# The attention stage of a macaron block: loops written out, the exponentials' scale in a register, another order of the maximum pass

## The chip, the cores and the metric

One NeuronCore of a Trainium2 chip runs the whole program. The time is device microseconds of one execution, first to last instruction plus the little that lies around them; the metric is the median of several executions.

## What is computed

x has 2 x 2048 tokens of width 256. The block is a half-weighted feed-forward layer, causal attention with 16 heads of 16, and the same feed-forward layer again, each behind a layer norm:

```python
x = x + 0.5 * ffn(layernorm(x))
x = x + attention(layernorm(x))      # B=2, S=2048, 16 heads of DK=16, causal, softmax, output projection + bias
x = x + 0.5 * ffn(layernorm(x))      # ffn: [x,-x] -> 1024 -> 1024 -> 256, weights +-1
```

## The kernel before

The program has three stages that share one set of PSUM tiles: A (first feed-forward layer, then q, k, v, which go to scratch memory in HBM), B (attention) and C (context and output projection, second feed-forward layer). The change is in stage B alone, which runs from about 475 to 1298 us of the span.

Stage B works on 16 pairs of heads (2 batches x 8). A pair has 4 query chunks of 512 (QCH); chunk i takes 2i+2 steps, 20 steps in all (STEPS): steps 0-1 are chunk 0, 2-5 chunk 1, 6-11 chunk 2, 12-19 chunk 3. A step has four slots j = 0..3: two key blocks of 128 times two heads. For each slot `scores` (L1201) makes four matmuls of 32 columns each side by side into one of three PSUM banks (`ffn_mm` 0 to 2), ACT makes the exponential (L1161) with a scale that it reads from SBUF, `exp_scale[:, 0:1]`, and writes `probs`. POOL masks the diagonal blocks (L1114). Three steps later (PV_LAG) `products` (L1222) multiplies the four slots with v in fp32 and adds into the fourth bank; PV_POINTS says after which slot of a step. When a chunk's last products are done, ACT copies the context out (L1150, `evacuate`) and SP stores it (L1066).

The softmax needs each row's maximum. It comes from a second pass over q and k, the maximum pass: 40 "units" of 128 queries x 512 keys a pair (`pe_item`, L568, and L573 for the diagonal's mask), into two PSUM tiles used in turn (`ffn_tr`, `ffn_acc`); DVE reduces each (L588, `dve_item`). After a chunk's last unit DVE makes the negated maxima as columns; a "turn" transposes them on PE (L577), DVE casts them to `m_row` (L601), and SP copies `m_row` into the two shift rows of q with two DMAs (`sp_rows`, L607). Turns are called T0 to T3 here, by chunk. `scores` of chunk i wait at their first slot for the rows of Ti: `rows_in`, 32 for each turn, counted over all pairs.

The maximum pass runs ahead: while pair p's scores run, the units of its later chunks and of pair p+1's first chunks are made. OWN_POINTS and AHEAD_POINTS say after which slot (4 x step + slot) each item comes; where products stand at the same slot, the item comes behind them. LEAD = 21 units of the first pair are made before stage B's scores begin.

q, k and v of pair p+1 come by `load_pair` (L302 to L305): 16 DMAs for q and k, one for v, into the other of two buffers, once the last products of pair p-1, which read that buffer, are done. SP works its queue in order. In one pair that order is written by hand: the rows of T2, then the load, then the stores and the other turns:

```python
order = [turns[0], "load", 0, 1, turns[1]] + turns[2:3] + [2] + turns[3:4] + [3]
for x in order:
    if x == "load":
        wait(sp, se.pv_done, pair * STEPS)
```

In the last pair the load is that of the first context chunk (`load_ctx`, 8 DMAs, L480), which DVE (`normalize`, L1279 to L1286) takes up behind its last turn; the second context chunk is loaded when that is done.

The code is a body of two pairs: body 0 stands alone, bodies 1 to 6 are a hardware loop on each engine (`Fori`), body 7 stands alone. In the loop, thresholds of semaphores are computed from the loop's register.

Of the kernel before, what the change touches and what calls it, by code (L numbers as in the profile page):

```python
# [22 lines left out]
U32 = mybir.dt.uint32  # L23
ALU = mybir.AluOpType
# [4 lines left out]
P = 128  # L29
# [4 lines left out]
CH = 512  # L34
# [15 lines left out]
BODY_PAIRS = 2  # L50
BODIES = BATCH * PAIRS // BODY_PAIRS
# [4 lines left out]
LEAD = 21  # L56
# [192 lines left out]
def build(nc, x, w_q, w_k, w_v, w_o, b_o, k0, k1, k2, s0, s1, s2, out):  # L249
# [8 lines left out]
    with ExitStack() as top:  # L258
# [239 lines left out]
        def with_turns(lo, hi):  # L498

            seq = []  # L500
            for n in range(lo, hi):
                seq.append(units[n])
                seq += [("turn", i) for i in range(QCH - 1) if last_unit[i] + TURN_DELAY[i] == n]
            return seq

        AHEAD = with_turns(0, LEAD)
        OWN = with_turns(LEAD, UNITS) + [("turn", QCH - 1)]
        assert len(AHEAD) == len(AHEAD_POINTS) and len(OWN) == len(OWN_POINTS)
        assert len(AHEAD) + len(OWN) == S_USES and S_USES % 2 == 0
# [17 lines left out]
        def schedule(u, last):  # L527

            plan = [[] for _ in range(4 * STEPS)]
            work = [(u, x) for x in OWN] + [(1 - u, x) for x in AHEAD]  # L530
            for use, ((buf, x), point) in enumerate(zip(work, OWN_POINTS + AHEAD_POINTS)):
                if buf == u or not last:
                    plan[point].append((buf, x, use))
            return plan

# [3 lines left out]
        body_steps = [(u, s) for u in range(BODY_PAIRS) for s in range(STEPS)]  # L539
        LOAD_STEP = AHEAD_POINTS[0] // 4  # L540
        OUT_PROJ_STEP = STEPS - 6
        EXPS, NSTEP = 4 * len(body_steps), len(body_steps)

        def bank(k):

            return 1 if k == EXPS - 1 else k % ST_BANKS

        def bank_free(k):

            return next(n for n in range(k - 1, k - EXPS, -1) if bank(n % EXPS) == bank(k)) + 1  # L550
# [503 lines left out]
        with ExitStack() as st:  # L1054
# [7 lines left out]
            @block.sync  # L1062
            def _(sp):
                def store(pair, n, i):
                    wait(sp, se.ctx_done, n + 1)
                    sp.dma_start(ctx_scr[bass.ds(pair, 1), :, i * CH:(i + 1) * CH].rearrange("o p n -> (o p) n"),  # L1066
                                 ctx_out[:, i % 2, :]).then_inc(ctx_st[i % 2], 16)

                def body(it, last):
                    for u in range(BODY_PAIRS):  # L1070
                        pair = it * BODY_PAIRS + u
                        base = pair * S_USES + len(AHEAD)
                        turns = [(b, x[1], use) for step in schedule(u, last and u == 1) for b, x, use in step if x[0] == "turn"]
                        order = [turns[0], "load", 0, 1, turns[1]] + turns[2:3] + [2] + turns[3:4] + [3]
                        for x in order:
                            if x == "load":
                                wait(sp, se.pv_done, pair * STEPS)
                                if last and u == 1:
                                    load_ctx(sp, 0, 0)
                                else:  # L1080
                                    load_pair(sp, 1 - u, pair + 1)
                                continue
                            if last and u == 1 and x == QCH - 2:
                                wait(sp, sc.ctx_n, 1)
                                load_ctx(sp, 0, 1)
                            if isinstance(x, int):
                                store(pair, pair * QCH + x, x)
                            else:
                                sp_rows(sp, x[0], x[1], base + x[2])
# [4 lines left out]
                body(0, False)  # L1094
                with sp.Fori(1, BODIES - 1) as it:
                    body(it, False)
                body(BODIES - 1, True)
                for sem in ctx_st:
                    sp.wait_ge(sem, 8 * BATCH * PAIRS * QCH)

            @block.gpsimd
            def _(pool):
                def body(it):
                    for g, (u, s) in enumerate(body_steps):
                        if not diagonal(s):
                            continue
                        i = chunk_of[s]
                        for par in range(2):
                            kb, _, c0 = step_slots(s)[2 * par]
                            w = (kb - TPC * i + 1) * P - c0  # L1110
                            pool.wait_ge(se.exp_done, it * EXPS + 4 * g + 2 * par + 2)
                            pool.sem_inc(se.gate_pool, 1)
                            view = probs[:, g % P_SLOTS, 2 * par:2 * par + 2, c0:c0 + w]
                            nc.gpsimd.affine_select(out=view, in_=view, compare_op=ALU.is_ge, fill=0.0,  # L1114
                                                    base=c0 - (kb - TPC * i) * P, pattern=[[0, 2], [1, w]],
                                                    channel_multiplier=-1).then_inc(se.mask_done, 1)

                with pool.Fori(0, BODIES - 1) as it:
                    body(it)
                body(BODIES - 1)  # L1120

            @block.vector
            def _(dve):
# [3 lines left out]
                def body(it, last):  # L1127
                    for u in range(BODY_PAIRS):
                        pair = it * BODY_PAIRS + u
                        for step in schedule(u, last and u == 1):  # L1130
                            for buf, x, use in step:
                                i = x[1] if x[0] == "turn" else x[1] // TPC
                                owner = pair if buf == u else pair + 1
                                dve_item(buf, x, pair * S_USES + len(AHEAD) + use, (len(AHEAD) + use) % 2, owner * QCH + i)

                with dve.Fori(0, BODIES - 1) as it:
                    body(it, False)
                body(BODIES - 1, True)

            @block.scalar  # L1140
            def _(act):
                ends = [g + PV_LAG for g, (u, s) in enumerate(body_steps) if s + 1 == STEPS or chunk_of[s + 1] != chunk_of[s]]

                def body(it, first=False, last=False):
                    def evacuate(n, body=0):

                        stored = BODY_PAIRS * QCH * 8
                        wait(act, se.pv_done, it * NSTEP + (body * NSTEP + ends[n] - PV_LAG + 1))
                        wait(act, ctx_st[n % 2], it * stored + (body * stored + n // 2 * 16))
                        nc.scalar.activation(ctx_out[:, n % 2, :], ctx_ps[:, :], ACT.Copy).then_inc(se.ctx_done, 1)  # L1150

                    for g, (u, s) in enumerate(body_steps):
                        for j, (kb, h, c0) in enumerate(step_slots(s)):
                            k = 4 * g + j
                            if first and k == 4 * (P_SLOTS - 1):
                                act.wait_ge(sa.qk_st, NCH * 128)
                                act.wait_ge(sa.v_st, NCH * 64)
                            if j == 0:
                                wait(act, se.pv_done, it * NSTEP + (g - P_SLOTS + 1))
                            wait(act, se.st_ready, it * EXPS + k + 1)  # L1160
                            nc.scalar.activation(probs[:, g % P_SLOTS, j, c0:CH], st_ps[bank(k)][:, c0:CH], ACT.Exp,  # L1161
                                                 scale=exp_scale[:, 0:1]).then_inc(se.exp_done, 1)
                            if j == PV_POINTS[s] and g in ends:
                                evacuate(ends.index(g))
                            if j == PV_POINTS[s] and g + NSTEP in ends and not first:
                                evacuate(ends.index(g + NSTEP), -1)
                    if last:
                        act_ln_sqrt(ln3, 0)
# [248 lines left out]
```

## Time and profile before

| | |
|---|---|
| median of 3 runs | 1689.33 us (1683.36 to 1690.95) |
| profiled execution, its own time | 1687.42 us |
| its span | 1685.7 us |
| PE busy | 1610.8 us (96%) |
| DVE busy | 1158.1 us (69%) |
| ACT busy | 948.2 us (56%) |
| mean granted TensorE clock | 0.984 |

In stage B PE, DVE and ACT are all near full in most slices of the span; outside it PE alone is. A busy PE is not PE at its peak: matmuls overlap, and so the distance between the starts of two of them, not their length, is what one costs.

### The profile page before, as it was taken

The numbers are of one execution on the slowest core, as the hardware profiler recorded it, in microseconds if no ns is written. First come the engines' busy times: TensorE is split into PE (matmuls) and PEld (weight loads), VectorE is DVE, ScalarE is ACT, GpSimd is POOL, SyncE is SP. The second block draws the span as 40 slices with busy tenths as digits, with TensorE's granted clock in tenths as the row PEclk, the third lists the DMA queues.
The fourth block names the chain that finished last, engine by engine and source line by source line (L and its number), as shares of the span: only waits on it lengthen the run. The fifth ranks groups of instructions, "written<-read, shape, count | busy, mean of one in ns | idle before, by whom it ended". The sixth has DMA issues, their size and how long they took to land.

```text
span 1685.7 us, 40071 instructions
## 1 busy us (share of the span) xinstructions
PE 1610.8 (96%) x14224; PEld 731.9 (43%) x14224; DVE 1158.1 (69%) x1746; ACT 948.2 (56%) x1703; POOL 160.1 (9%) x320
## 2 busy tenths in 40 slices
PE   6899999999989999898999999999997899999998
PEld 3455555555533333333333333333332455555554
DVE  6545543454589888787887878878886556666632
ACT  2223223232279999797997989889997222222211
POOL 5200000000011111111111111111110000000000
PEclk9999999999999999999999999999999899999999
DMA  5011013110131112220122202222213111113000
GB/s 172 0 51 50 0 50 87 50 36 14 49 104 50 37 51 65 59 65 26 49 65 59 65 30 51 59 60 63 59 44 102 51 51 50 50 50 110 15 12 13
DMA packets 115790, 89.42 MB, mean 53 GB/s; under 512 B 76080, under 2 KB 95152, under 8 KB 115632
## 3 DMA queue, kind: packets, MB, share of 16 engines
q1 hardware_dynamic: 115632, 87.20, 18.0%
q8 instruction: 113, 1.85, 0.5%
q14 instruction: 45, 0.37, 0.1%
HBM read 49.15 MB, written 37.75 MB: 52 GB/s over the span
## 4 chain that ended last, share of the span: by engine, by line
PE 87%; DVE 3%; issue 3%; ACT 2%; DMA 2%; SPq 2%; DVEq 0%; ACTq 0%
PE ffn_mm L400 26%; PE ffn_mm L1201 16%; PE ffn_mm L1222 13%; PE ffn_mm L388 7%; PE ffn_acc L416 7%; PE ffn_acc L568 5%; PE ffn_tr L568 5%; PE ffn_mm L667 3%; PE ffn_acc L679 2%; ACT probs L1161 2%; PE ffn_acc L488 1%; PE ffn_tr L375 1%; PE ffn_tr L573 1%; DVE qk L1282 1%; DMA qk<-ctx_scr 1%
## 5 line engine op out<-in xcount | busy, mean ns | idle before, releaser
L1161 ACT ACTIVATE probs<-ffn_mm,exp_scale 128x512 f32<-128x512 f32 (+3 forms) x1280 | 705.5, 641 | 96.4 <-PE ffn_mm L1201 90.7
L1201 PE MATMUL ffn_mm<-qk 66*32 66x512 f16 (+7 forms) x5120 | 413.5, 359 | 25.2 <-issue 19.9
L588 DVE TENSOR_REDUCE m_part<-ffn_acc 128x2 f32<-128x1024 f32 (+1 forms) x314 | 351.2, 1119 | 76.4 <-PE ffn_acc L568 44.1
L400 PE MATMUL ffn_mm<-ffn_h1h,w 128*128 128x512 f16 x1024 | 389.4, 380 | 7.5 <-DVE ffn_h2l L453 7.5
L400 PE MATMUL ffn_mm<-ffn_h1l,w 128*128 128x512 f16 x1024 | 389.2, 380 | 0.0
L588 DVE TENSOR_REDUCE m_part<-ffn_tr 128x2 f32<-128x1024 f32 (+3 forms) x326 | 328.0, 1006 | 28.6 <-PE ffn_tr L573 15.4
L1222 PE MATMUL ffn_mm<-probs,v 128*32 128x512 f32 (+3 forms) x2560 | 307.7, 538 | 2.3
L446 ACT ACTIVATE ffn_h2h<-ffn_mm 128x512 f16<-128x512 f32 x128 | 76.2, 598 | 309.2 <-PE ffn_mm L400 294.5
L1201 PEld LDWEIGHTS ffn_mm<-qk 66*32 66x32 f16 (+1 forms) x5120 | 131.5, 94 | 252.3 <-ACT probs L1161 136.0
L453 DVE SCALAR_TENSOR_TENSOR ffn_h2l<-ffn_mm,ffn_h2h 128x512 f16<-128x512 f32 x128 | 86.3, 688 | 188.5 <-ACT ffn_h2h L446 188.5
L1114 POOL TENSOR_SCALAR_AFFINE_SELECT probs<-probs 128x256 f32<-128x256 f32 (+1 forms) x256 | 108.0, 422 | 734.8 <-ACT probs L1161 734.6
L400 PEld LDWEIGHTS ffn_mm<-ffn_h1h,w 128*128 128x128 f16 x1024 | 100.5, 98 | 126.0 <-DVE ffn_h2l L453 8.0
L446 ACT ACTIVATE ffn_h1h<-ffn_mm 128x512 f16<-128x512 f32 x128 | 76.5, 598 | 139.8 <-PE ffn_mm L388 139.8
L400 PEld LDWEIGHTS ffn_mm<-ffn_h1l,w 128*128 128x128 f16 x1024 | 100.5, 98 | 117.9 <-issue 1.3
L568 PE MATMUL ffn_acc<-qk 64*128 64x512 f16 (+1 forms) x628 | 117.3, 370 | 3.6 <-DVE m_part L588 2.8
L568 PE MATMUL ffn_tr<-qk 64*128 64x512 f16 (+3 forms) x652 | 114.5, 346 | 0.5
L416 PE MATMUL ffn_acc<-w,ffn_h2h 128*128 128x256 f16 x512 | 113.8, 273 | 0.3 <-DVE ffn_h2l L453 0.3
L416 PE MATMUL ffn_acc<-w,ffn_h2l 128*128 128x256 f16 x512 | 113.7, 273 | 0.0
L453 DVE SCALAR_TENSOR_TENSOR ffn_h1l<-ffn_mm,ffn_h1h 128x512 f16<-128x512 f32 x128 | 88.6, 692 | 35.6 <-ACT ffn_h1h L446 35.1
L388 PE MATMUL ffn_mm<-ffn_xh,w 128*128 128x512 f16 x256 | 99.3, 388 | 3.5 <-DVE ffn_xl L432 2.4
L388 PE MATMUL ffn_mm<-ffn_xl,w 128*128 128x512 f16 x256 | 99.2, 388 | 0.0
L1222 PEld LDWEIGHTS ffn_mm<-probs,v 128*32 128x32 f32 x2560 | 74.4, 110 | 32.9 <-ACT ctx_out L1150 8.1
(99 smaller groups left out, 1104.9 us busy)
## 6 DMA issues: line engine op xcount, KB each, us to landing
qk<-qk_scr SPq DMA_DIRECT2D x256, 64.0 KB, 2.6
ctx_scr<-ctx_out SPq DMA_DIRECT2D x64, 256.0 KB, 2.8
qk<-ctx_scr SPq DMA_DIRECT2D x64, 256.0 KB
v_scr<-v_pad SPq DMA_DIRECT2D x32, 256.0 KB, 2.9
v<-v_scr SPq DMA_DIRECT2D x16, 512.0 KB, 4.6
x_res<-L_attn_x SPq DMA_DIRECT2D x8, 512.0 KB, 3.8
qk_scr<-qk_hi SPq DMA_DIRECT2D x32, 128.0 KB, 1.8
qk_scr<-qk_lo SPq DMA_DIRECT2D x32, 128.0 KB, 1.8
```

Source lines behind the costliest of these rows:

```text
L388: ins = nc.tensor.matmul(f.mm[:, m % 4, :], w0[:, kt, m * P:(m + 1) * P], part[:, kt, :], start=(kt == 0 and part is f.xh), stop=(kt == DT ...
L400: ins = nc.tensor.matmul(f.mm[:, m % 4, :], w1[:, kt, m * P:(m + 1) * P], part[:, kt, :], start=(kt == 0 and part is f.h1h), stop=(kt == H ...
L416: ins = nc.tensor.matmul(f.acc[:, t // 2, t % 2 * D:(t % 2 + 1) * D], part[:, kt, t * P:(t + 1) * P], w2[:, kt, :], start=(kt == 0 and par ...
L446: nc.scalar.activation(dst[:, m, :], f.mm[:, m % 4, :], ACT.Relu).then_inc(hi, 1)
L453: nc.vector.scalar_tensor_tensor(out=dst[:, m, :], in0=f.mm[:, m % 4, :], scalar=0.0, in1=src[:, m, :], op0=ALU.max, op1=ALU.subtract).the ...
L568: ins = nc.tensor.matmul(s_ps[slot][:, h, 0:w], q_part(u, h, HEAD_ROWS[h], slice(t * P, (t + 1) * P)), k_part(u, h, HEAD_ROWS[h], slice(r ...
L588: nc.vector.tensor_reduce(m_part[u][:, t, :, r], s_ps[slot][:, :, 0:w], AX.X, ALU.max).then_inc(sb.s_done, 1)
L667: ins = nc.tensor.matmul(f.mm[:, j, :], w_t[:, j // DT, kt, j % DT * P:(j % DT + 1) * P], src[:, kt, :], start=(kt == 0), stop=(kt == DT - 1))
L1114: nc.gpsimd.affine_select(out=view, in_=view, compare_op=ALU.is_ge, fill=0.0, base=c0 - (kb - TPC * i) * P, pattern=[[0, 2], [1, w]], chan ...
L1161: nc.scalar.activation(probs[:, g % P_SLOTS, j, c0:CH], st_ps[bank(k)][:, c0:CH], ACT.Exp, scale=exp_scale[:, 0:1]).then_inc(se.exp_done, 1)
L1201: ins = nc.tensor.matmul(st_ps[bank(k)][c:c + 32, c0:CH], k_part(u, h, rows, slice(kb * P + c, kb * P + c + 32)), q_part(u, h, rows, slice ...
L1222: ins = nc.tensor.matmul(ctx_ps[row:row + 32, c0:CH], v_buf[u][:, kb, h * 32:(h + 1) * 32], probs[:, g % P_SLOTS, j, c0:CH], start=start, ...
```

## The change

- Stage B's hardware loops are gone: on every engine the 16 pairs are written out, and all semaphore thresholds are constants.
- ACT loads the scale once into a register, and the exponentials take it from there.
- The maximum pass has one table of 44 points for a pair. A point is 2 x (4 x step + slot) + late; an item with late = 0 comes ahead of the products of that slot, one with late = 1 behind them. LEAD is 24 (26 items are made ahead in place of 23), TURN_DELAY has a fourth number, PV_POINTS are others.
- SP has no order by hand: it goes through steps and slots, and at each slot first come the rows of a turn of that slot, then a store, then, at step 2's products, the load.

```diff
-LEAD = 21
+LEAD = 24
-PV_POINTS = (3, 1, 2, 1, 1, 0, 2, 1, 2, 1, 3, 2, 2, 1, 1, 0, 1, 2, 2, 2)
-TURN_DELAY = (2, 7, 3)
-OWN_POINTS = (1, 2, 3, 8, 9, 12, 13, 15, 15, 16, 19, 21, 22, 25, 27, 28, 29, 31, 33, 34, 39)
-AHEAD_POINTS = (39, 41, 41, 44, 46, 47, 51, 52, 52, 54, 56, 57, 59, 62, 63, 66, 68, 68, 71, 73, 75, 77, 77)
+PV_POINTS = (1, 1, 2, 1, 2, 1, 3, 2, 3, 2, 2, 0, 1, 0, 1, 0, 2, 2, 3, 1)
+TURN_DELAY = (2, 7, 4, 3)
+ITEM_POINTS = (5, 5, 14, 20, 22, 24, 24, 28, 32, 37, 41, 48, 49, 55, 55, 61, 67, 73, 73, 76, 77, 78, 78, 85,
+              89, 94, 95, 102, 102, 107, 111, 118, 119, 126, 129, 129, 138, 138, 143, 145, 145, 152, 152, 159)
...
+                for pair in range(ALL_PAIRS):
+                    last = pair == ALL_PAIRS - 1
+                    for s in range(STEPS + (PV_LAG if last else 0)):
+                        g = pair * STEPS + s
+                        for j in range(4):
+                            for _, owner, x, use in items(pair, s, j) if s < STEPS else ():
+                                if x[0] == "turn":
+                                    sp_rows(sp, owner % 2, x[1], use)
+                            if j == PV_POINTS[s % STEPS] and g in ends:
+                                n = ends.index(g)
+                                if last and n == len(ends) - 2:
+                                    wait(sp, sc.ctx_n, 1)
+                                    load_ctx(sp, 0, 1)
+                                store(n // QCH, n, n % QCH)
+                            if j == PV_POINTS[s % STEPS] and s == PV_LAG - 1:
+                                wait(sp, se.pv_done, pair * STEPS)
+                                if last:
+                                    load_ctx(sp, 0, 0)
+                                else:
+                                    load_pair(sp, 1 - pair % 2, pair + 1)
...
+                scale_now = act.alloc_register("exp_scale")
+                act.reg_load(scale_now, exp_scale[0:1, 0:1].bitcast(U32))
...
-                            nc.scalar.activation(probs[:, g % P_SLOTS, j, c0:CH], st_ps[bank(k)][:, c0:CH], ACT.Exp,
-                                                 scale=exp_scale[:, 0:1]).then_inc(se.exp_done, 1)
+                        nc.scalar.activation(probs[:, g % P_SLOTS, j, c0:CH], st_ps[bank(k)][:, c0:CH], ACT.Exp,
+                                             scale=scale_now).then_inc(se.exp_done, 1)
...
+                for g in range(ALL_STEPS):
+                    pair, s = divmod(g, STEPS)
+                    for j in range(4):
+                        scores(g, j)
+                        max_pass(pair, s, j, 0)
+                        if j == PV_POINTS[s] and g >= PV_LAG:
+                            products(g - PV_LAG)
+                        max_pass(pair, s, j, 1)
```

## Rows read from the trace of the kernel before

**Rows 1.** The windows view: pair 1, pairs 3 to 12, pair 14: length, busy by engine, PEclk.
```profile
526.18:575.41 49.23, 48.93 (x628) 17.50 (x624) 43.55 (x57) 45.43 (x86) 6.75 (x16) 1.00 0.20 56
625.60:1149.13 523.53, 501.36 (x6284) 178.05 (x6280) 435.67 (x561) 455.01 (x841) 67.47 (x160) 0.97 0.20 53
1198.44:1247.94 49.50, 49.12 (x632) 17.59 (x632) 43.39 (x57) 45.57 (x85) 6.75 (x16) 1.00 0.24 55
```

**Rows 2.** PE's timeline in a stretch without idle time.
```profile
824.30 0.39 PE L568 MATMUL ffn_acc<-qk 64*128 64x512 f16 x2
824.62 0.40 PE L1201 MATMUL ffn_mm<-qk 128*32 128x512 f16 x4
...
825.75 1.03 PE L1222 MATMUL ffn_mm<-probs,v 128*32 128x512 f32 x8
826.61 0.39 PE L1201 MATMUL ffn_mm<-qk 66*32 66x512 f16 x4
...
827.75 0.39 PE L568 MATMUL ffn_tr<-qk 64*128 64x512 f16 x2
827.98 0.38 PE L568 MATMUL ffn_acc<-qk 64*128 64x512 f16 x2
```

**Rows 3.** ACT's timeline where it runs without a break.
```profile
804.52 3.00 ACT L1161 ACTIVATE probs<-ffn_mm,exp_scale 128x512 f32<-128x512 f32 x5 [0.82 <-PE ffn_mm L1201]
807.39 0.62 ACT L1150 ACTIVATE ctx_out<-ffn_mm 128x512 f32<-128x512 f32 x1
807.87 5.51 ACT L1161 ACTIVATE probs<-ffn_mm,exp_scale 128x512 f32<-128x512 f32 x10
```

**Rows 4.** DVE's timeline, reductions one behind the other.
```profile
855.77 1.22 DVE L588 TENSOR_REDUCE m_part<-ffn_acc 128x2 f32<-128x1024 f32 x1
856.90 1.22 DVE L588 TENSOR_REDUCE m_part<-ffn_tr 128x2 f32<-128x1024 f32 x1
```

**Rows 5.** PE's timeline behind two idle stretches: start, length, instructions, idle before.
```profile
783.07 1.04 PE L1201 MATMUL ffn_mm<-qk 66*32 66x512 f16 x8 [4.37 <-issue]
...
1311.71 1.97 PE L375 MATMUL ffn_tr<-ident,ln_xn 128*128 128x128 f32 x8 [12.16 <-DVE ln_xn L367]
...
1320.64 0.38 PE L388 MATMUL ffn_mm<-ffn_xl,w 128*128 128x512 f16 x1
```

**Rows 6.** The view by line and form, stage B, ACT: busy us, mean ns.
```profile
L1161 ACT ACTIVATE probs<-ffn_mm,exp_scale 128x512 f32<-128x512 f32 x912 | 557.6, 703 | 48.6 <-PE ffn_mm L1201 47.0
...
L1150 ACT ACTIVATE ctx_out<-ffn_mm 128x512 f32<-128x512 f32 x63 | 38.6, 613 | 0.0
```

**Rows 7.** SP's queue in a pair of the loop and in pair 14.
```profile
842.01 0.35 SPq L1066 DMA_DIRECT2D ctx_scr<-ctx_out  x1
...
845.35 0.36 SPq L303 DMA_DIRECT2D qk<-qk_scr  x1
...
854.12 0.40 SPq L305 DMA_DIRECT2D v<-v_scr  x1
...
1207.41 1.30 SPq L607 DMA_DIRECT2D qk<-m_row  x2
1208.76 0.39 SPq L303 DMA_DIRECT2D qk<-qk_scr  x1
...
1216.13 0.42 SPq L305 DMA_DIRECT2D v<-v_scr  x1
```

**Rows 8.** PE's timeline of that loop pair: step 2's products.
```profile
840.35 0.60 PE L1222 MATMUL ffn_mm<-probs,v 128*32 128x256 f32 x7
```

**Rows 9.** The source view of L305: from issue to landing of v's load.
```profile
DMA to landing us min/median/max: 4.2/4.6/5.3
```

**Rows 10.** The chain of waits: landing of one turn's rows.
```profile
777.74 1.64 DMA qk<-m_row
```

**Rows 11.** A context load in SP's queue, and DVE's timeline where it is waited for.
```profile
1282.33 5.13 SPq L480 DMA_DIRECT2D qk<-ctx_scr  x8
...
1299.27 1.23 DVE L1279 TENSOR_TENSOR qk<-qk 128x1024 f32<-128x1024 f32 x1 [10.08 <-DMA qk<-ctx_scr]
```

More of the change, by code:

```diff
@@ L496, in build @@
         last_unit = {i: max(n for n, x in enumerate(units) if x[1] // TPC == i) for i in range(QCH)}
[L498 to L509, printed above, removed]
+        PERIOD, due = [], []
+        for n in range(2 * UNITS):
+            PERIOD.append((n // UNITS, units[n % UNITS]))
+            due += [(n + TURN_DELAY[i], n // UNITS, i) for i in range(QCH) if last_unit[i] == n % UNITS]
+            PERIOD += [(d, ("turn", i)) for at, d, i in due if at == n]
+        PERIOD = PERIOD[PERIOD.index((0, units[LEAD])):PERIOD.index((1, units[LEAD]))]
+        AHEAD = [x for d, x in PERIOD if d == 1]
+        assert len(PERIOD) == S_USES and len(ITEM_POINTS) == S_USES and S_USES % 2 == 0
         chunk_of = [i for i in range(QCH) for _ in range(2 * i + 2)]
@@ L525, in step_slots, with items @@
             return out
[L527 to L534, printed above, removed]
         def diagonal(s):
             return chunk_of[s] * TPC <= step_slots(s)[0][0]
-        body_steps = [(u, s) for u in range(BODY_PAIRS) for s in range(STEPS)]
-        LOAD_STEP = AHEAD_POINTS[0] // 4
+        ALL_STEPS = ALL_PAIRS * STEPS
         OUT_PROJ_STEP = STEPS - 6
-        EXPS, NSTEP = 4 * len(body_steps), len(body_steps)
+        EXPS = 4 * STEPS
+        def items(pair, s, j):
+            found, use = [], len(AHEAD) + pair * S_USES
+            for (d, x), point in zip(PERIOD, ITEM_POINTS):
+                if pair + d == ALL_PAIRS:
+                    continue
+                if point // 2 == 4 * s + j:
+                    found.append((point % 2, pair + d, x, use))
+                use += 1
+            return found
+        ends = [pair * STEPS + s + PV_LAG for pair in range(ALL_PAIRS) for s in range(STEPS)
+                if s + 1 == STEPS or chunk_of[s + 1] != chunk_of[s]]
         def bank(k):
-            return 1 if k == EXPS - 1 else k % ST_BANKS
+            return k % ST_BANKS
         def bank_free(k):
-            return next(n for n in range(k - 1, k - EXPS, -1) if bank(n % EXPS) == bank(k)) + 1
+            return k - ST_BANKS + 1
         EARLY = [0] * 15 + [1] * 3 + [0]
@@ L1067, in store @@
                                  ctx_out[:, i % 2, :]).then_inc(ctx_st[i % 2], 16)
[L1069 to L1089, printed above, removed]
                 sp_rows(sp, 0, 1, AHEAD.index(("turn", 1)))
@@ L1136, in _ @@
-                with dve.Fori(0, BODIES - 1) as it:
-                    body(it, False)
-                body(BODIES - 1, True)
+                for pair in range(ALL_PAIRS):
+                    for s in range(STEPS):
+                        for j in range(4):
+                            for _, owner, x, use in items(pair, s, j):
+                                i = x[1] if x[0] == "turn" else x[1] // TPC
+                                dve_item(owner % 2, x, use, use % 2, owner * QCH + i)
@@ L1140, in _ @@
             @block.scalar
             def _(act):
[L1142 to L1160, printed above, removed]
-                            nc.scalar.activation(probs[:, g % P_SLOTS, j, c0:CH], st_ps[bank(k)][:, c0:CH], ACT.Exp,
-                                                 scale=exp_scale[:, 0:1]).then_inc(se.exp_done, 1)
[L1163 to L1168, printed above, removed]
-                        for n, g in enumerate(ends):
-                            if g >= NSTEP:
-                                evacuate(n)
@@ L1178, in _ @@
+                act_ln_sqrt(ln3, 0)
+                evacuate(len(ends) - 1)
             @block.tensor
@@ L1249, in _, with scores @@
-                body(0, first=True)
-                with pe.Fori(1, BODIES - 1) as it:
-                    body(it)
-                body(BODIES - 1, last=True)
+                def scores(g, j):
+                    pair, s = divmod(g, STEPS)
+                    i = chunk_of[s]
+                    kb, h, c0 = step_slots(s)[j]
+                    k = 4 * g + j
+                    if j == 0 and s == first_step[i]:
+                        wait(pe, se.rows_in, (pair * QCH + i + 1) * 32)
+                    wait(pe, se.exp_done, bank_free(k))
+                    rows = ALL_ROWS[h]
+                    for c in range(0, P, 32):
+                        ins = nc.tensor.matmul(st_ps[bank(k)][c:c + 32, c0:CH], k_part(pair % 2, h, rows, slice(kb * P + c, kb * P + c + 32)),
+                                               q_part(pair % 2, h, rows, slice(i * CH + c0, (i + 1) * CH)), start=True, stop=True,
+                                               tile_position=(0, c))
+                    ins.then_inc(se.st_ready, 1)
@@ new lines, in max_pass @@
+                def max_pass(pair, s, j, after):
+                    for late, owner, x, use in items(pair, s, j):
+                        if late != after:
+                            continue
+                        if owner != pair and x == units[0]:
+                            load_wait(owner % 2, owner // 2)
+                        pe_item(owner % 2, x, use % 2, use - 1, owner * QCH + x[1] + 1 if x[0] == "turn" else None)
+                for g in range(ALL_STEPS):
+                    pair, s = divmod(g, STEPS)
+                    for j in range(4):
+                        scores(g, j)
[3 more added lines that the diff above has]
+                        max_pass(pair, s, j, 1)
+                    if pair == ALL_PAIRS - 1 and s == OUT_PROJ_STEP:
+                        wait(pe, se.s_done, ALL_PAIRS * S_USES)
+                        pe_out_proj(pe, 0, lambda j: None)
@@ L1255, in build @@
+                for g in range(ALL_STEPS - PV_LAG, ALL_STEPS):
+                    products(g)
         with ExitStack() as st:
@@ L1360, in free @@
                         elif m < ST_BANKS:
-                            wait(pe, sb.exp_done, BODIES * EXPS)
+                            wait(pe, sb.exp_done, ALL_PAIRS * EXPS)
                         else:
```

137 lines of the change are left out of this document (48 added, 89 removed).

## The prediction

> **What bounds the kernel now.** I looked first at the windows view, cut at the first exponential of each pair. A pair of straight code takes 49.2 to 49.5 us at full clock; PE is busy for 48.9 of them, DVE for 43.6, ACT for 45.4 [rows 1]. Three engines are close together, so the limit must be read from distances between starts. In PE's timeline a product step of 512 columns lasts until the next start 0.86 us, which is four passes of 0.215; a unit lasts 0.22 when another unit follows and 0.32 when a score does [rows 2]: going from a score or product to a unit, or back, costs 0.10 more each way. ACT's exponential of 512 columns costs (807.39 - 804.52)/5 = 0.574, its context copy 0.48 [rows 3]. DVE's full reduction costs 1.13 [rows 4].
>
> PE's floor for a pair: scores 58 slots of 512, 6 of 384, 8 of 256 and 8 of 128 columns, 14.7 us; products, 16 steps at 0.86 and 4 at 0.43, 15.5; units 28 x 0.215 + 12 narrow ones of 0.11 on average, 7.3; masks 16 x 0.11, 1.8; together 39.3. Laid out slot by slot, the tables before have 76 crossings between units and the rest: + 7.6 = 46.9. ACT's floor, each form at its length less the overlap of 0.13, is 58 x 0.574 + 6 x 0.47 + 8 x 0.35 + 8 x 0.24 + 4 copies x 0.48 = 42.7 (the narrower forms by 0.11 a 128 columns); DVE's is its busy 43.6 less the overlap of its records (1.22 long, 1.13 apart [rows 4]), about 42.3. Of 49.3, some 2.4 are then waits of PE where ACT or DVE is late for a moment.
>
> **The loops.** Ten pairs of the loop with five jumps back take 523.5 us [rows 1]; ten straight ones would take 493. The jumps cost 30.5: PE stands idle 4.37 us, waiting for nothing but its own issue [rows 5], and the granted clock falls behind it: 0.97 over these pairs, 1.00 over a straight one [rows 1]. Written out, the code has no jump, and straight pairs in the bodies at both ends show no such hole: -30.5. Register arithmetic on the queues goes too; it is hidden behind work.
>
> **The register.** The exponential that reads its scale from SBUF lasts 703 ns, the context copy of the same shape, without an operand in SBUF, 613 [rows 6], and the starts differ by the same 0.09 [rows 3]. No row has a scale from a register. Bounds: nothing saved, or 0.09 each; I take 0.09, since a register is known before the engine starts. ACT's floor falls by 80 x 0.09 to 35.6, and ACT is out of the way but for three chunk ends. The load of the register stands once on ACT, behind the table load, while PE is busy with the units ahead: nothing.
>
> **The new order.** The new tables have 13 places where a unit follows a unit (before 5) and 62 crossings (before 76): PE's floor is 39.3 + 6.2 = 45.5. DVE's 42.3 must fit into that with two tiles between. I went along the 44 items with 1.13 for each full reduction: at three places a unit is one or two tenths late. With ACT's chunk ends I take 0.5 of waits: 46.0 a pair, 3.2 less than now, for 15 pairs -48. The last pair ends by its last turn and the chain behind it; the turn comes 3 us earlier: -3. LEAD = 24 makes three more units before the first scores, at DVE's 1.13 [rows 4]: +3.4. So far 1687.4 - 30.5 - 48 - 3 + 3.4 = 1609.
>
> **What is moved on SP's queue.** This decides. ITEM_POINTS gives T2 the point 22, which is step 2, slot 3. The load hangs on step 2's products, at slot PV_POINTS[2] = 2. So SP now has the load ahead of T2's rows; before it had them the other way round [rows 7]. Scores wait for T2's rows at step 6. Counted from the pair's first score:
> - By the floors steps 0 to 5 take 2.4, 1.6, 1.7, 2.8, 2.05 and 1.6. Step 0, for example: two scores 0.44, products 0.86, a score and the crossing 0.32, two units 0.22 + 0.32, a score 0.22. PE is at step 6 at 12.2 us.
> - Step 2's products start behind three scores and a narrow unit, 1.0 into the step, at 5.0. The store of the context follows them by 842.01 - 840.35 = 1.66 [rows 7, 8] and takes 0.4: the load starts at 7.1.
> - Its 17 DMAs hold SP until v's issue, 8.8 us later (854.12 - 845.35), or 7.4 in pair 14 (1216.13 - 1208.76) [rows 7]. That lands 4.6 later [rows 9], at 20.5.
> - T2's two DMAs come behind. If they must follow v's data, they land at about 20.7. If they overtake it, v is issued by 16.4, they take 1.3 [rows 7] and land 1.64 later [rows 10], at 19.3, or at 17.9 with the load of 7.4.
>
> By the Trainium skill, "DMA: Bandwidth & Descriptors", section "Queues, rings and completion order", SP has one row of rings, and descriptors of a ring are consumed in order. By that rule it is 20.7; no row shows rows of a turn behind a load. Left to the rows, I take a landing of 20 to 20.7, as no row shows a later DMA of SP overtaking a load's: PE waits 8 us. PE, ACT and DVE are all idle then, since every engine's work hangs on scores; nothing hides it. Then the clock: 4.4 us of idle cost some 1.6 beyond the idle, and after 12.2 us of idle PE was slow from 1311.7 to 1320.6 [rows 5], half of that lost, 4.4. For 8 us of idle I take 2.4 between these, less 0.4 for waits that the pause clears: 10.0 a pair. Pairs 1 to 14: +140. In pair 0 the load needs no wait and is under way before the scores: +1. In the last pair the load in T2's way is the context's, 8 DMAs of 256 KB, which are waited for until 1299.3 when issued at 1282.3 [rows 11], 17 us: T2's rows land at 7.1 + 17.2 = 24.3, PE waits 12, with the clock 14, and the chain behind T3 moves by that: +14.
>
> The load's own due time doesn't bind: q and k are in some 3 us behind their last issue, at 18 to 19, and pair p+1's first unit stands in step 9, which begins at 19.3 without the wait.
>
> Sum: 1609 + 140 + 1 + 14 = 1764. The medians lie 1.9 above this execution: 1766.
>
> **The rivals.** (a) T2's rows overtake the load's data: the wait is 5.7 to 7.1, net about 8 a pair, and 4 in the last: 1609 + 112 + 1 + 4 + 2 = 1728. For it: 2 KB DMAs use few rings. Against it: these rings carry the load too. (b) The other side: T2's rows are in time. It decides at the landing of 12.2; SP would have to be through with the load in under 3 us in place of 8.8. The two loads read took SP 8.8 and 7.4 us, so only a mistake of mine about SP's order leads there. Then 1609 + 2 = 1611. (c) The register saves nothing: ACT's waits of about 1 us a pair stay, 1781. (d) The clock stays low longer after each wait, at the upper bound: 14 x 2 more, 1794.
>
> **How the numbers follow.** The rows in order: 0.57. (a) 0.19, (b) 0.13, (c) 0.07, (d) 0.04. The rows' case alone spans 1745 to 1785. The range goes from 1718, under (a), to 1790, above (c): it leaves out (b), (d) and the outermost tails. Half a per cent, about 8 us, is what a measurement of this kernel can tell from no change: faster 0.13, same 0.02, slower 0.85.
>
> **What would show it.** Right: in each pair one idle stretch of PE of 6 to 8 us at the first score of step 6, released by the DMA of `m_row`; SP's queue with 17 loads ahead of two row copies; PEclk below 1 after it; exponentials of 613 ns; no hole at pair ends; without the stretch 46 us a pair. Wrong: no such stretch, a shorter load, or pairs of more than 47 us beside it.

## The result, and the profile after

The changed kernel takes 1772.15 us (median of 4 runs, 1770.89 to 1774.0); the kernel before, on the same chip, 1686.34 (4 runs). The ratio is 1.049, 95% interval 1.047 to 1.051: slower by 86 us between the two medians (79 to 86 by the interval). The forecast was 1766 us. The profiled execution took 1774.0 us, its span is 1772.2, PE is busy for 1609.3 us of it (91%), DVE 1156.7, ACT 851.0 (48%), and the mean granted clock is 0.951.

The windows view, cut at the first exponential of a pair, answers [rows 1]: pairs 0, 1, 3, 14 and 15 of the kernel after.

```profile
480.29:529.24 48.95, 48.46 (x612) 17.32 (x608) 43.11 (x57) 39.05 (x83) 6.45 (x16) 0.92 0.19 50
529.24:585.87 56.63, 49.19 (x636) 17.88 (x632) 43.39 (x57) 39.47 (x84) 6.62 (x17) 0.94 0.19 48
643.41:701.06 57.65, 49.79 (x636) 17.91 (x632) 43.56 (x57) 39.47 (x84) 6.62 (x17) 0.91 0.19 47
1270.97:1328.79 57.82, 50.09 (x636) 18.00 (x632) 43.55 (x57) 39.47 (x85) 6.62 (x17) 0.91 0.20 47
1328.79:1387.07 58.28, 46.58 (x550) 17.23 (x546) 34.29 (x41) 38.76 (x84) 7.03 (x16) 0.91 0.26 92
```

Pair 0 has no load to wait for and takes 48.95. Pairs 1 to 14 take 55.7 to 58.0 each; the three of them shown here have a granted clock of 0.91 to 0.94. The exponentials and the context copies answer [rows 6] (view by line and form):

```profile
L1143 ACT ACTIVATE probs<-ffn_mm 128x512 f32<-128x512 f32 x928 | 500.4, 608 | 250.1 <-PE ffn_mm L1172 241.4
...
L1131 ACT ACTIVATE ctx_out<-ffn_mm 128x512 f32<-128x512 f32 x64 | 40.1, 627 | 1.0 <-PE ffn_mm L1192 1.0
```

With the scale in a register an exponential lasts 608 ns in place of 703, a little less than the copy: 95 ns saved, forecast 90. The Trainium skill, "ScalarE: Activation LUTs", section "What ACT_TABLE_LOAD costs", gives 93 ns for each operand that is a [128,1] pointer; these two rows agree with it.

SP's queue in pair 14, from the store ahead of the load on, answers [rows 7]:

```profile
1277.09 0.34 SPq L1064 DMA_DIRECT2D ctx_scr<-ctx_out  x1
1277.48 0.52 SPq L302 DMA_DIRECT2D qk<-qk_scr  x1
...
1286.22 0.42 SPq L304 DMA_DIRECT2D v<-v_scr  x1
1286.68 1.61 SPq L605 DMA_DIRECT2D qk<-m_row  x2
```

From issue to landing of v's load, the source view of L304, as in [rows 9]:

```profile
DMA to landing us min/median/max: 4.3/4.5/5.0
```

And PE's timeline in the same stretch:

```profile
1282.92 0.29 PE L1172 MATMUL ffn_mm<-qk 66*32 66x128 f16 x8
1290.76 0.62 PE L1172 MATMUL ffn_mm<-qk 66*32 66x512 f16 x4 [7.55 <-DMA qk<-m_row]
...
1293.64 1.93 PE L1192 MATMUL ffn_mm<-probs,v 128*32 128x512 f32 x8
```

DVE's timeline:

```profile
1291.97 1.23 DVE L586 TENSOR_REDUCE m_part<-ffn_acc 128x2 f32<-128x1024 f32 x1 [8.27 <-PE ffn_acc L566]
```

PE's waits summed over the whole program (us, times, the longest):

```profile
PE ffn_mm L1172 <- DMA qk<-m_row: 112.6, 15, 8.8
```

The piece of the chain of waits that answers [rows 10], from the start of the second row's issue to its landing:

```profile
1287.68 3.04 DMA qk<-m_row
```

In [rows 10] the same piece is 1.64. Had the rows landed that fast, they would have been in at 1289.32: some 6.1 us of the pause come from the late issue alone, behind 17 others on SP, and 1.4 from the slower landing. This split is an estimate from these two rows.

This is the predicted picture. SP has the 17 DMAs of the load ahead of T2's two rows; PE reaches step 6 at 1283.21, which is 12.24 us into the pair (forecast 12.2), and stands until the rows are in. It happens 15 times and sums to 112.6 us. DVE has nothing to do either. Behind the pause a product step lasts 1.93 us, not 1.03 [rows 2]: the granted clock is at half. The windows view of this pair shows it. The first line is step 6, the stretch behind the pause, with a PEclk of 0.50; the second is the pause; the third is the rest of the pair, at 0.99.

```profile
1290.76:1296.46 5.70, 5.70 (x36) 1.35 (x36) 2.40 (x3) 2.18 (x4) 0.00 (x0) 0.50 0.00 0
1283.20:1290.76 7.56, 0.01 (x3) 0.00 (x0) 0.50 (x1) 0.45 (x2) 0.66 (x2) 0.76 0.68 157
1297.00:1328.79 31.79, 31.61 (x431) 12.09 (x427) 28.40 (x40) 26.03 (x55) 3.05 (x8) 0.99 0.05 18
```

The idle stretches at the jumps [rows 5] are gone: no later pair shows one.

In the last pair the context's load is in the way, answering [rows 11]; SP's queue:

```profile
1335.30 6.05 SPq L479 DMA_DIRECT2D qk<-ctx_scr  x8
1341.40 1.38 SPq L605 DMA_DIRECT2D qk<-m_row  x2
```

PE's timeline:

```profile
1349.83 0.62 PE L1172 MATMUL ffn_mm<-qk 66*32 66x512 f16 x4 [8.80 <-DMA qk<-m_row]
```

And the chain of waits, from the start of the second row's issue:

```profile
1342.12 7.67 DMA qk<-m_row
```

### The profile page after: what moved, and what is told of

Read it like the earlier page. It is cut to its first block, busy times and chain, and to the rows that moved or that the text cites. A ratio compares the mean times of both kernels' runs of the same rounds, so it can differ in the third digit from the quotient of the medians.

```text
span 1772.2 us, 36023 instructions
## 1 busy us (share of the span) xinstructions
PE 1609.3 (91%) x14224; PEld 735.7 (42%) x14224; DVE 1156.7 (65%) x1746; ACT 851.0 (48%) x1703; POOL 160.0 (9%) x320
## 4 chain that ended last, share of the span: by engine, by line
PE 81%; SPq 8%; DMA 4%; DVE 3%; ACT 2%; issue 1%; ACTq 0%; DVEq 0%
PE ffn_mm L399 24%; PE ffn_mm L1172 14%; PE ffn_mm L1192 12%; PE ffn_mm L387 6%; PE ffn_acc L415 6%; PE ffn_acc L566 5%; PE ffn_tr L566 4%; SPq L302 3%; PE ffn_mm L665 3%; SPq L303 3%; DMA qk<-m_row 3%; PE ffn_acc L677 2%; PE ffn_acc L487 1%; ACT probs L1143 1%; PE ffn_tr L374 1%
## 5 line engine op out<-in xcount | busy, mean ns | idle before, releaser
L1143 ACT ACTIVATE probs<-ffn_mm 128x512 f32<-128x512 f32 (+3 forms) x1280 | 608.8, 547 | 282.4 <-PE ffn_mm L1172 273.5
L1172 PE MATMUL ffn_mm<-qk 66*32 66x512 f16 (+7 forms) x5120 | 401.6, 368 | 115.0 <-DMA qk<-m_row 112.6
L586 DVE TENSOR_REDUCE m_part<-ffn_acc 128x2 f32<-128x1024 f32 (+2 forms) x345 | 368.0, 1067 | 193.6 <-PE ffn_acc L566 183.6
L586 DVE TENSOR_REDUCE m_part<-ffn_tr 128x2 f32<-128x1024 f32 (+3 forms) x295 | 310.7, 1053 | 21.0 <-PE ffn_tr L571 11.2
L1192 PE MATMUL ffn_mm<-probs,v 128*32 128x512 f32 (+3 forms) x2560 | 314.6, 550 | 0.6 <-POOL probs L1106 0.5
L1172 PEld LDWEIGHTS ffn_mm<-qk 66*32 66x32 f16 (+1 forms) x5120 | 123.1, 96 | 339.1 <-DMA qk<-m_row 115.3
L566 PE MATMUL ffn_acc<-qk 64*128 64x512 f16 (+2 forms) x690 | 130.5, 373 | 5.9 <-DVE m_part L586 3.2
L566 PEld LDWEIGHTS ffn_acc<-qk 64*128 64x128 f16 x690 | 36.1, 93 | 151.6 <-issue 148.4
```

The lines of the kernel that those rows point to most:

```text
L566: ins = nc.tensor.matmul(s_ps[slot][:, h, 0:w], q_part(u, h, HEAD_ROWS[h], slice(t * P, (t + 1) * P)), k_part(u, h, HEAD_ROWS[h], slice(r ...
L586: nc.vector.tensor_reduce(m_part[u][:, t, :, r], s_ps[slot][:, :, 0:w], AX.X, ALU.max).then_inc(sb.s_done, 1)
L1172: ins = nc.tensor.matmul(st_ps[bank(k)][c:c + 32, c0:CH], k_part(pair % 2, h, rows, slice(kb * P + c, kb * P + c + 32)), q_part(pair % 2, ...
L1192: ins = nc.tensor.matmul(ctx_ps[row:row + 32, c0:CH], v_buf[pair % 2][:, kb, h * 32:(h + 1) * 32], probs[:, g % P_SLOTS, j, c0:CH], start= ...
```

## The experiments

The theory: SP's order costs some 10 us a pair; without it the rest of the change makes the kernel faster, by the loops, the register and the order of the maximum pass. Rivals: the loss belongs to the new order of the maximum pass itself, or to the load's traffic, not to its place in SP's queue.

**SP's order alone.** The change, with T2's rows ahead of the load on SP:

```diff
                                 if x[0] == "turn":
                                     sp_rows(sp, owner % 2, x[1], use)
+                                if x == ("turn", 2):
+                                    wait(sp, se.pv_done, pair * STEPS)
+                                    if last:
+                                        load_ctx(sp, 0, 0)
+                                    else:
+                                        load_pair(sp, 1 - pair % 2, pair + 1)
...
-                            if j == PV_POINTS[s % STEPS] and s == PV_LAG - 1:
-                                wait(sp, se.pv_done, pair * STEPS)
...
```

> The kernel after, with one thing changed: SP issues the rows of T2 first and the load (in the last pair the context load) right behind them. Theory (the load ahead of T2's rows costs each pair a pause of about 7.5 us and the clock behind it): no pause at step 6; a pair takes what it takes now without the pause, 47.3 us by its steps; time 1772 - 14 x 9.8 - 12 = 1623 us. Rival (the load is what the queue is about, and later it is late itself): PE waits at step 9 for q and k, 1 to 2 us a pair, 1640 to 1650 us. If the pause is of another cause, the time stays at 1772.

Measured: 1625.39 us (ratio to before 0.962, interval 0.960 to 0.965). SP's queue:

```profile
865.59 0.34 SPq L1064 DMA_DIRECT2D ctx_scr<-ctx_out  x1
865.97 1.26 SPq L605 DMA_DIRECT2D qk<-m_row  x2
867.28 0.39 SPq L302 DMA_DIRECT2D qk<-qk_scr  x1
...
875.68 0.42 SPq L304 DMA_DIRECT2D v<-v_scr  x1
```

And the pair, windows view:

```profile
859.47:906.82 47.35, 47.07 (x636) 17.67 (x632) 43.38 (x57) 39.28 (x84) 6.62 (x17) 1.00 0.21 58
```

The pause is gone and the clock is full. The 147 us between the two versions of the change hang on which of the two SP has first. Of the kernels here that do the whole of the work this one is the fastest, 3.8% below the kernel before.

**Which of the other parts gives what.** Three more kernels with T2's rows first: with the scale from SBUF again; with the old tables and LEAD 21 but the register; and with both old, so that only the loops are gone.

```diff
-                                             scale=scale_now).then_inc(se.exp_done, 1)
+                                             scale=exp_scale[:, 0:1]).then_inc(se.exp_done, 1)
```

```diff
-LEAD = 24
+LEAD = 21
-PV_POINTS = (1, 1, 2, 1, 2, 1, 3, 2, 3, 2, 2, 0, 1, 0, 1, 0, 2, 2, 3, 1)
+PV_POINTS = (3, 1, 2, 1, 1, 0, 2, 1, 2, 1, 3, 2, 2, 1, 1, 0, 1, 2, 2, 2)
...
-TURN_DELAY = (2, 7, 4, 3)
+TURN_DELAY = (2, 7, 3, 0)
...
```

ITEM_POINTS become the old points of both tables, each as 2 x point + 1, so that items stand behind the products as before.

> e1_rows_first with the exponentials' scale read from SBUF as before. Theory (0.09 us less for each exponential, worth something only where ACT is the later one): exponentials of 512 columns back at 703 ns, a pair about 48.3 us, 1 us more than with the register; time about 1638 us. Rival (PE's order alone sets the pair): the same time as e1_rows_first within 3 us.

> e1_rows_first with the old order of the maximum pass and of the products, and LEAD 21; loops written out, scale in the register. Theory (14 crossings more a pair at 0.10 us): a pair takes 47.3 + 1.2 = 48.5 us, less the 3.4 us of the three units ahead at the start; time about 1638 us. Rival (the order is worth nothing, since DVE and ACT set the pair): the same time as e1_rows_first or less.

> Only the loops written out: old order, scale from SBUF, T2's rows ahead of the load. Theory (five jumps of about 6 us go, nothing else): pairs of 49.2 us, no idle stretch at pair ends; 1686 - 30.5 = 1656 us. Rival (code that is written out brings stalls of its own in the fetch of instructions): above 1665 us with PE waits put down to issue.

Measured: 1651.67, 1643.38 and 1650.38 us, where 1638, 1638 and 1656 were expected. The first is the miss: beside the new order the register is worth 1.61 us a pair, not 1. One pair of each, windows view; new order and SBUF:

```profile
871.42:920.38 48.96, 48.09 (x636) 17.69 (x632) 43.71 (x57) 45.46 (x85) 6.72 (x17) 1.00 0.21 56
```

Old order and register:

```profile
865.98:914.54 48.56, 48.12 (x632) 17.38 (x628) 43.45 (x57) 40.14 (x85) 6.73 (x16) 1.00 0.20 56
```

Old order and SBUF, only the loops gone:

```profile
870.65:919.67 49.02, 48.76 (x632) 17.51 (x628) 43.53 (x57) 45.34 (x85) 6.72 (x16) 1.00 0.20 56
```

Per pair: old order and SBUF 49.02, old order and register 48.56, new order and SBUF 48.96, both new 47.35. The register alone is worth 0.46 us, the order alone 0.06, the two together 1.67. The waits of PE over the whole program say why. New order, scale in SBUF:

```profile
PE ffn_mm L1169 <- ACT probs L1140: 5.6, 28, 0.4
```

Old order, register:

```profile
PE ffn_acc L574 <- DVE m_col L594: 5.1, 16, 0.3
```

With the scale in SBUF it is ACT that PE waits for, 28 times visibly; with ACT fast and the old tables a turn comes too early for DVE's columns, 16 times. That each edit takes away a limit behind which the other stands is how I read these rows; beyond the four pair times it wasn't tested. The waits that can be seen are a small part of it: 5.6 us in all with the scale in SBUF and 1.7 with it in the register, where the kernels differ by 26.

The loops: 15 pairs take 739.16 us in the kernel with nothing but the loops gone, and 772.48 before (from 475.46 to 1247.94), so the loops cost 33.3 in these pairs, forecast 30.5. Of that, 19.9 is PE's idle time at the five jumps, 3.1 to 4.4 each ([rows 5] has one of them).

**The register in the kernel before**, loops and old tables kept:

```diff
+                scale_now = act.alloc_register("exp_scale")
+                act.reg_load(scale_now, exp_scale[0:1, 0:1].bitcast(U32))
...
-                                                 scale=exp_scale[:, 0:1]).then_inc(se.exp_done, 1)
+                                                 scale=scale_now).then_inc(se.exp_done, 1)
```

> The kernel before with the scale in a register and nothing else. Theory (the register gives ACT 7 us a pair, but in the old order PE's floor of 46.9 and DVE stand in the way; written out, the same step took a pair from 49.02 to 48.56): 0.46 x 15 = 7 us less, about 1680 us. Rival (it is worth in any order what it was worth in the new one, 1.6 us a pair): 1662 us.

Measured: 1673.17 us (6 runs, ratio 0.992, interval 0.989 to 0.995), 14 us faster, between the two expectations. Ten pairs of the loop, to be set beside the 523.53 of [rows 1]:

```profile
624.33:1140.37 516.04, 498.50 (x6284) 177.49 (x6280) 435.47 (x561) 402.06 (x842) 67.17 (x160) 0.98 0.20 54
```

That is 0.75 a pair on average; the kernel without loops gave 0.46. But it isn't spread evenly: the five pairs that end with a jump save 6.8 us together and the five others 0.7, and PE's idle time at the jumps falls from 19.9 to 15.3. So in the old order the register gives well under 1 us a pair in either form of the code, and in the loop most of it shows up at the jumps. Why the jumps cost less wasn't looked at.

**The same fault in the kernel before.** The loops, the tables and the SBUF scale stay; only SP's order in a body is turned round:

```diff
-order = [turns[0], "load", 0, 1, turns[1]] + turns[2:3] + [2] + turns[3:4] + [3]
+order = ["load", turns[0], 0, 1, turns[1]] + turns[2:3] + [2] + turns[3:4] + [3]
```

> The kernel before (loops, scale from SBUF, old order) with one line changed: in SP's order by hand the load stands ahead of T2's rows. Theory: the same pause at the first score of step 6, in a kernel that has nothing else of the change. The load starts 2 us after step 2's products, which begin at 5.9, so at 8.0; v lands 13.3 later, T2's rows with it, at 21.5; step 6 was reached at 14.1: a pause of 7.4 us and 2.2 for the clock, less in the pairs where a jump's low clock lies before it. About 1687 + 14 x 9.5 + 10 = 1830 us. Rival (the pause needs the faster pairs of the new order, the old one has room): under 1720 us.

Measured: 1836.06 us (2 runs, ratio 1.088, interval 1.084 to 1.092), 149 us above before. The order of the queue does the same harm without any other part of the change; PE in one pair:

```profile
732.66 1.05 PE L1201 MATMUL ffn_mm<-qk 66*32 66x512 f16 x8 [8.53 <-DMA qk<-m_row]
```

**Half of the load ahead.** The change, with T2's rows behind 8 of the 17 DMAs (the last pair as in the change):

```diff
         def load_pair(sp, u, pair, between=None):
...
+                if h == 1 and between:
+                    between()
```

> The kernel after, with T2's two row copies put in the middle of the load, behind 8 of its 17 DMAs (not in the last pair, which stays as it is). Theory (the rows land when what is ahead of them on SP's queue has been issued and has landed): the load starts at 7.3, eight issues take 3.7, the rows 1.3, landing at 14.5 to 15.5 instead of 20.2: a pause of 2 to 3 us where it was 7.5, and less lost to the clock; a pair 50 to 51 us, about 1675 us. Rival (any load in flight delays the rows alike, by sharing the DMA engines): a pause near 7.5 us, about 1765 us.

Measured: 1647.05 us (2 runs, ratio 0.976, interval 0.973 to 0.980). SP's queue:

```profile
870.58 0.43 SPq L304 DMA_DIRECT2D qk<-qk_scr  x1
...
874.29 1.27 SPq L607 DMA_DIRECT2D qk<-m_row  x2
875.61 0.39 SPq L304 DMA_DIRECT2D qk<-qk_scr  x1
```

PE's timeline:

```profile
876.96 0.40 PE L1175 MATMUL ffn_mm<-qk 66*32 66x512 f16 x4 [0.64 <-DMA qk<-m_row]
```

And the chain of waits, from the start of the second row's issue:

```profile
874.95 1.96 DMA qk<-m_row
```

I had expected 1675 and was wrong on the landing. Behind eight DMAs of q and k (64 KB each) the rows are in 2.67 us after their first issue, and the piece of the chain is 1.96, only 0.3 more than in [rows 10]; the pause is 0.64, the granted clock stays at 1.00 and the pair takes 48.10. A pause of this size costs little beyond itself: 48.10 - 47.35 = 0.75. The last pair still pauses, for 7.75 us, and takes 56.7.

**The queue or the traffic.** The change with the load where it is, but T2's rows issued on ACT's queue in step 3:

```diff
+                        if s == 3 and j == 1:
+                            use2 = next(u for _, o, x, u in items(g // STEPS, 2, 3) if x == ("turn", 2))
+                            sp_rows(act, g // STEPS % 2, 2, use2)
```

> The kernel after, with the load ahead on SP as it is, but T2's rows issued by ACT on its own queue, behind the second exponential of step 3. Theory (it is SP's queue that holds the rows, not the load's traffic): the rows land at 9 to 12 us of the pair, before step 6; no pause. ACT pays two issues of 0.65 us a pair, of which PE may feel up to 1 us: 1625 to 1640 us. Rival (the load's data fill the DMA engines, whatever queue the rows take): the rows still land near v, the pause stays, 1765 us or so.

Measured: 1628.53 us (4 runs, ratio 0.965, interval 0.962 to 0.968). ACT's queue:

```profile
869.69 0.62 ACTq L605 DMA_DIRECT2D qk<-m_row  x1
```

SP's load in the same pair begins here:

```profile
869.38 0.43 SPq L302 DMA_DIRECT2D qk<-qk_scr  x1
```

PE goes from step 5 into step 6 (12 matmuls in the first line, the last four of them step 6's) without a pause:

```profile
874.89 0.55 PE L1175 MATMUL ffn_mm<-qk 66*32 66x128 f16 x12
875.37 0.39 PE L566 MATMUL ffn_acc<-qk 64*128 64x512 f16 x2
```

And the pair, windows view:

```profile
862.88:910.27 47.39, 47.17 (x636) 17.70 (x632) 43.40 (x57) 39.20 (x84) 6.65 (x17) 1.00 0.22 58
```

The load is where the change has it, and the loss is gone: a load that is issued and moved while the rows are on their way doesn't hold them. What costs the time is that the rows are issued behind it on SP. What this run doesn't tell is whether rows issued late, with the whole load on its way, would be quick on another queue: here they are issued when one or two of its DMAs are out. So the 1.4 us of slower landing in the change may come from the order in the queue or from shared traffic; no run here parts the two.

**Why a pair takes 47.35 and not 46.0.** Three kernels on the version with T2's rows first: reductions over half of their columns; exponentials over half of theirs in pairs 1 to 15; and both.

```diff
-nc.vector.tensor_reduce(m_part[u][:, t, :, r], s_ps[slot][:, :, 0:w], AX.X, ALU.max)
+nc.vector.tensor_reduce(m_part[u][:, t, :, r], s_ps[slot][:, :, 0:w // 2], AX.X, ALU.max)
```

```diff
+                        c1 = CH if g < STEPS else c0 + (CH - c0) // 2
-                        nc.scalar.activation(probs[:, g % P_SLOTS, j, c0:CH], st_ps[bank(k)][:, c0:CH], ACT.Exp,
+                        nc.scalar.activation(probs[:, g % P_SLOTS, j, c0:c1], st_ps[bank(k)][:, c0:c1], ACT.Exp,
```

> e1_rows_first with each reduction of the maximum pass in the attention stage reading only the first half of its unit's columns (so the maxima are of half the keys); PE's and ACT's work is unchanged. A pair of e1 takes 47.35 us where the floor that I counted for PE is 45.5. If the missing 1.9 are waits for PSUM tiles that DVE holds (I counted some 1.2 at the second units of couples, the rest at the ends of chunks where ACT's context copy is late), a pair falls to about 46.1 and the kernel to 1605 or so. Rival: the floor itself is short by 1.9 and PE is the bound throughout: a pair stays at 47.3 and the kernel within 5 us of e1's 1625. If DVE was behind all of it: 45.5, 1595.

> e1_rows_first with the exponentials of pairs 1 to 15 over half their columns (the other half of probs keeps what an earlier pair left), so ACT has about half its work; PE's and DVE's are unchanged. If ACT costs PE only the moments at the ends of chunks, a pair falls by 0.4 to 0.7 us from 47.35 and the kernel to about 1616; if the register has taken ACT out of the way altogether, nothing changes (1625); if ACT is still the larger part of the missing 1.9, it falls by more than 1.2 and the kernel to 1606 or less.

> e1_rows_first with both cuts: the attention stage's reductions read half of their unit's columns in all pairs, and the exponentials of pairs 1 to 15 half of theirs. Neither DVE nor ACT should then hold PE anywhere, and what a pair takes is PE's own floor. Pairs took 47.35 us in e1, 46.43 with short reductions alone, 47.11 to 47.25 with short exponentials alone. If my floor of 45.5 is right, ACT's delays come to light only once DVE is out of the way, and a pair falls to 45.5 (kernel about 1597). If the floor is short by some 0.7, a pair stays between 46.1 and 46.4 (kernel 1606 to 1610).

Measured: 1610.48, 1624.57 and 1605.17 us (2 runs each; ratios 0.953, 0.962 and 0.950, each within 0.007). A pair of each, windows view; short reductions:

```profile
849.34:895.77 46.43, 46.43 (x636) 17.30 (x632) 26.49 (x57) 39.21 (x84) 6.62 (x17) 1.00 0.21 59
```

Short exponentials:

```profile
859.57:906.82 47.25, 46.91 (x636) 17.60 (x632) 43.34 (x57) 26.23 (x85) 6.65 (x17) 1.00 0.22 58
```

Both:

```profile
845.91:891.93 46.02, 46.02 (x636) 17.05 (x632) 26.50 (x57) 26.22 (x85) 6.63 (x17) 1.00 0.23 59
```

These kernels leave out half of the columns of the reductions, of the exponentials or of both, and serve only to take the times. With both shortened a pair takes 46.02, and PE is busy in all of it. I take this as PE's floor, though what is measured is that the floor isn't above it; 45.5 was then 0.5 too low. DVE holds PE for 47.35 - 46.43 = 0.92; ACT for 0.41 once DVE is away (46.43 - 46.02), and for only 0.1 to 0.2 while DVE is there (pairs of 47.11 to 47.25), too little to move the kernel's time: 1624.57 against 1625.39. Where DVE does it can be seen in PE's timeline at the same couple of units. With whole reductions:

```profile
871.86 0.39 PE L566 MATMUL ffn_acc<-qk 64*128 64x512 f16 x2
872.35 0.34 PE L566 MATMUL ffn_tr<-qk 64*128 64x384 f16 x2
```

With short ones:

```profile
861.61 0.39 PE L566 MATMUL ffn_acc<-qk 64*128 64x512 f16 x2
861.83 0.33 PE L566 MATMUL ffn_tr<-qk 64*128 64x384 f16 x2
```

The second unit comes 0.49 behind the first, where 0.22 is what PE needs: its tile is still being reduced. Such a wait is too short for the timeline to print one in brackets, and PE counts as busy meanwhile. The last pair took 51.3, 49.5 and 49.8 us in the three, against 47.3; I didn't look into that.

## Why the prediction was right, and where it was off

Term by term; "measured" is the profiled execution after, or the difference of two of the kernels above.

| term | forecast us | measured us | from |
|---|---|---|---|
| loops | -30.5 | -33.3 | pairs 0 to 14, loops gone against before |
| register and order, 15 pairs | -48 | -27.4 | 711.75 (T2's rows first) - 739.16 (loops gone) |
| rows behind the load, pairs 1 to 14 | +140 | +136.7 | 799.55 after - 662.88 with T2's rows first |
| pair 0 | +1 | +0.1 | 48.95 - 48.88 |
| LEAD, up to the first exponential | +3.4 | +4.8 | 480.29 - 475.46 |
| last pair | -3 + 14 | +8.4 | 58.28 - 49.91 |
| behind the last pair | 0 | -2.7 | 385.1 - 387.8 |
| sum on 1687.4 | 1764 | 1774.0 | |

**The step that decided held.** SP's order was read right from the tables, and the times in it too: the load starts 6.5 us into the pair (7.1 forecast), v is issued 8.7 later (8.8) and lands 4.46 later, at 19.7 (20.5); the pauses of pairs 1 to 14 are 6.5 to 7.9 us, 7.42 on average (8 forecast). Of 136.7/14 = 9.76 a pair, 2.34 are then more than the pause, where the forecast had 2.4 for the clock less 0.4 for waits that the pause would clear. Pair by pair this rest goes from 1.4 to 2.9. In pair 14 it is 2.9: step 6 takes 5.70 us at half clock where it takes 3.35 without a pause, and the first scores of step 7 take another 0.4 more, since the clock is back only behind 1297. Why it is smaller in other pairs, and whether any wait was cleared, wasn't looked at.

**Rival (a), the rows overtake the load's data, falls.** It put the last pair's pause at about 4. There the rows land 7.67 us after the start of the second issue, against 1.64 with nothing ahead [rows 10], and PE stands 8.8. In pair 14 the rows are in at 1290.72 and v, issued ahead of them, at 1286.22 + 4.46 = 1290.68. By the Trainium skill, "DMA: Bandwidth & Descriptors", section "Queues, rings and completion order", descriptors of a ring are consumed in order and the semaphore's write comes only behind the earlier writes of that DMA engine; these two rows agree. The rival's price was also a little too high: the 1.64 begins with the second issue, so it must not stand behind the 1.3 of both, and its landing is 18.7, not 19.3, which takes some 9 us from its 1728. **Rival (b)**, rows in time, is what the kernel with T2's rows first makes true (1625, forecast 1611). **Rival (c)**, the register saves nothing, is refuted on both counts: 95 ns an exponential, and 26.3 us of kernel time between the new order with and without it, more than the 15 that I gave it. **Rival (d)**, a longer slow clock, asked for 2 us more in each pair and falls by the 2.34.

**Mis-sized: a pair beside the pause.** I had 45.5 and 0.5 of waits, 46.0 together, and named pairs of more than 47 us as a sign of error; they take 47.35. The floor is 46.0 (+0.5), the waits 1.33 in place of 0.5, and 0.9 of them are DVE's. I had gone along the items with 1.13 for each reduction and found three late places of 0.1 to 0.2; one place alone has 0.27. So the term of -48 was -27, and it alone is 20.6 us of error. The loops (-2.8), the pause (-3.3), the last pair (-2.6) and the part behind it (-2.7) made half of it good, and that is luck: the mechanism was right, but the sum came nearer than its terms. The part behind the last pair takes 382 to 388 us in the kernels of this study, with loops and without, so its -2.7 is scatter. The same holds for some of the 4.8 of LEAD: kernels that differ in the order of the maximum pass and LEAD alone are 2.4 and 3.6 apart at their first exponential.

**Last pair.** The pause was 8.8, not 12: the context's 8 DMAs and T2's rows were in 14.5 us after the first issue. My 17 from [rows 11] is what the context load took there: DVE stood waiting and took the data up 0.14 us after the last landing, at 1299.13. In the kernel after, the same 8 DMAs have all landed at 1349.96, 14.7 after their first issue. So the transfer itself was 2.1 us shorter; why wasn't looked at.

## What to carry to other kernels

When a schedule is generated in place of an order by hand, read for each queue what now stands ahead of the smallest transfer that somebody waits for: here 2 rows behind a 17-DMA load turned a gain of 64 us (1625.39 against 1689.67) into a loss of 86, and one `if` brings it back. An operand taken from an engine's way and a better order of its neighbours may each give next to nothing (0.46 and 0.06 us a pair) and together 1.67, so try them together before either is dropped. A busy engine in the profile may be waiting for a tenth or a quarter of a microsecond at many places; shortening the suspected other engine's work for one run shows what it costs.

## What the runs showed of the hardware

- A scale in a register costs an exponential nothing that can be seen: 608 ns, where the scale from SBUF costs 703.
- SP needs 0.46 us from one DMA issue to the next. From the first of 17 to the last it is 7.4 to 8.9 us in the kernel after; in most loads one issue in the middle takes longer (1.1 to 1.9 us).
- From the start of the second row's issue, two rows land after 1.64 us with nothing ahead, 1.96 behind 8 DMAs of 64 KB, 3.04 behind the whole load with v's 512 KB, and 7.67 behind 8 DMAs of 256 KB. So once issued they are held by how much is queued ahead more than by the number of DMAs: 8 large ones hold them far longer than 8 small ones. The number counts before that, in the time until SP can issue them.
- Behind a pause of 7.55 us PE has a granted clock of 0.50 for 5.7 us and a little more; behind a pause of 0.64 us it stays at 1.00.
- A jump back of the loops costs 3.1 to 4.4 us of PE's idle time in the kernel before (2.8 to 3.8 with the scale in a register); with the lower clock behind them and all else that the loops change, five jumps come to about 33 us.
